# Softmax shifts with the logarithm of the row sum, taken on ScalarE ahead of the weighted sums, in a fused attention and FFN kernel

## The chip, the core and the metric

The kernel runs on one core of a Trainium2 chip. A core has TensorE (PE), VectorE (DVE), ScalarE (ACT), GpSimd (POOL) and SyncE (SP, which issues DMAs here); each works through its own list of instructions in order, and they meet only through semaphores. The metric is the time of one execution on the device in microseconds (us), lower is better. Some 0.3% (3.5 us) is about what a measurement of this kernel can tell.

## The reference, cut to what matters

```
x:(16,256,512)  ctx:(16,256,512)   HEADS=16, DK=32, WINDOW=128
q = rope(layernorm(x) @ wq.T);  k = rope(ctx @ wk.T);  v = ctx @ wv.T
scores = q @ k.T * sqrt(32), masked where |q - k| > 128
x = x + (softmax(scores) @ v) @ wo.T + wo_b
x = x + ffn(layernorm(x))      # W_in and W_out rounded to 8 bits, activations to 16; exact gelu
```

## The kernel before

**Phases.** Up to about 700 us of the profile the attention runs, 16 steps, one for each batch element b of 256 tokens; then the two FFN products. Only the attention is changed. All products there are done in split precision: an operand is a high part (rounded) and a low part (the rest), and `split3` makes three matmuls of each product. q and k of a head have 32 rows; high and low parts stand under one another (96 rows, `q_st`, `k_st`), so that one matmul gives scores of a head.

**A step.** `step(b)` on each engine is written out by hand, and this order is what runs. In a first half PE computes `scores(b, n)` for each head n (queries down the partitions), DVE masks them and takes each row's maximum (`row_maxima`, line 1224, two operations per head and a read of the result), and between them PE computes the projections of the next element: k (`qk_tile(b + 1, "k", ...)`, four pieces of 12 matmuls), the transposes of x (`x_transposes`, L529), V in two tiles of four triples (`v_tile`, L514 to L516), q (four pieces). Then the maxima are split and transposed (L620) and placed under the 96 rows of `q_st`, so that the same product subtracts them. In a second half PE computes the scores transposed (`scores_t`, L642), ACT takes the exponential (L973), POOL zeroes the corners outside the window (`band`, L1565), and after every four heads PE sums the values weighted (`weighted`, L656) and, with a one-hot operand, the denominators (`denominators`, L669). The output product of element b - 1 (`o_products`, 24 matmuls: for each half of the tokens eight with the high part, L589, and four with the low part, L593) is strewn through the end of the first half and the second half by `some(count)`.

**Denominators.** In the next step DVE inverts the sums (L1265), ACT issues two DMAs that spread them (`store_sums`, `spread_shares`), and DVE multiplies `oT` by them (L1271) before `ot_lead` (ACT, L950) and `ot_rest` (POOL, L1553) split it for the output product.

**Waits that matter.** PE has two score banks (`ring`): `scores(b, n)` waits until head n - 2 has left its bank. `v_tile(j, 0)` writes bank 6, which also holds the second half of x transposed, so it waits for `xt_lo`, the semaphore of `xt_rest` on DVE (L1257); `xt_rest` waits for `xt_lead` on ACT (L933). The k rotation on DVE (`rotate`, L1247 to L1250, three operations per half) ends in `roped`, from which ACT rounds k's high part (L913) and POOL makes the low part in four pieces (L1542); the part of `o_products` with the low part waits for `ot_rest`. The first thing that ACT does in a step is `norm1` (L929). SP stacks q and k by DMA when their parts are there.

## Time and profile before

| | |
|---|---|
| three runs | 1176.55 us median (1173.67 to 1177.44) |
| profiled execution | 1176.49 us, span of its instructions 1174.8 us |
| busy: PE, DVE, ACT, POOL | 1135.5 us (97%), 946.8 (81%), 646.8 (55%), 375.7 (32%) |
| granted TensorE clock, mean | 0.988 of full |
| chain that ended last, largest shares | PE 44%, DVE 26%, issue 25% |

A busy PE is not PE at its peak, since matmuls overlap: a row's length is the latency of one, and its pace is the distance of starts. The mean over the span also mixes the attention with the FFN phases, so one step of the attention has to be cut out.

### The profile page before, as it was taken

To read this page: it belongs to the slowest core of one execution; us is meant where nothing else is said; L and a number is where in the kernel's file an instruction comes from. 1 tells how busy PE (TensorE), PEld (TensorE's weight loads), DVE (VectorE), ACT (ScalarE), POOL (GpSimd) and SP (SyncE) were. 2 spreads that over 40 slices of the span, in tenths; PEclk is the share of its full clock that TensorE was granted. 3 is DMA by queue.
4 is the path that set the end of the run, shared out by engine and by line. 5 is a ranking of instruction groups with operands and counts; after the bars stand their busy time and mean duration, and the time that the engine had idled before them with its cause. 6 is when DMAs were issued, how large, how long until landed. Compare 5 with 4: busy or idle time off the path is not lost.

```text
span 1174.8 us, 23540 instructions
## 1 busy us (share of the span) xinstructions
PE 1135.5 (97%) x7928; PEld 766.9 (65%) x7928; DVE 946.8 (81%) x2413; ACT 646.8 (55%) x1033; POOL 375.7 (32%) x540
## 2 busy tenths in 40 slices
PE   6999999999999999999999789999999999999998
PEld 6867887887788788778878464444444444444443
DVE  6879989999999999999998756666666687777776
ACT  5255356436534643563464255555555577777774
POOL 1247337534743663474365230000000021111121
PEclk9989999999999999999999799999999999999999
DMA  8554674566457556646753723555553402676662
GB/s 281 133 150 114 172 221 118 148 184 163 126 175 212 129 137 184 172 123 179 203 139 92 222 65 118 197 196 198 196 196 117 152 1 77 214 232 227 224 216 99
DMA packets 100522, 191.10 MB, mean 163 GB/s; under 512 B 13376, under 2 KB 30912, under 8 KB 100416
## 3 DMA queue, kind: packets, MB, share of 16 engines
q1 hardware_dynamic: 96096, 179.92, 50.9%
q10 hardware_dynamic: 4320, 9.83, 2.8%
q8 instruction: 59, 0.97, 0.4%
q14 instruction: 47, 0.39, 0.1%
HBM read 89.16 MB, written 43.91 MB: 113 GB/s over the span
## 4 chain that ended last, share of the span: by engine, by line
PE 44%; DVE 26%; issue 25%; DMA 2%; ACT 1%; SPq 1%; DVEq 0%; POOL 0%; POOLq 0%; ACTq 0%
PE bank L864 19%; DVE bank L1224 12%; PE bank L642 6%; PE bank L656 5%; PE bank L669 5%; DVE row_max L1224 3%; PE bank L589 3%; PE bank L593 2%; DVE neg_max L1265 2%; DVE roped L1250 2%; DVE rt L1248 2%; DVE rt L1247 1%; DVE neg_max L1229 1%; DVE t_lo L1257 1%; PE bank L608 1%
## 5 line engine op out<-in xcount | busy, mean ns | idle before, releaser
L1224 DVE CUSTOM_DVE_ANT_0 bank<-bank,mask 128x256 f32<-128x256 f32 x512 | 203.5, 453 | 33.9 <-PE bank L608 23.1
L864 PE MATMUL bank<-wout_int,g_hi 128*128 128x512 bf16 x512 | 193.6, 379 | 0.1
L864 PE MATMUL bank<-wout_int,g_lo 128*128 128x512 bf16 x512 | 193.6, 379 | 0.0
L825 PE MATMUL bank<-qT_hi,win_int 128*128 128x512 bf16 x496 | 188.0, 379 | 0.0
L825 PE MATMUL bank<-qT_lo,win_int 128*128 128x512 bf16 x496 | 188.0, 379 | 0.0
L973 ACT ACTIVATE probs<-bank 128x512 f32<-128x512 f32 x256 | 139.0, 599 | 37.0 <-PE bank L642 31.1
L1542 POOL TENSOR_TENSOR k_lo<-roped,k_hi 128x256 fp32r<-128x256 f32 x60 | 55.0, 947 | 263.5 <-ACT k_hi L913 263.5
L1520 DVE TENSOR_TENSOR g_lo<-h_int,g_hi 128x512 f16<-128x512 f32 x128 | 89.1, 696 | 41.3 <-ACT g_hi L1129 37.4
L1565 POOL TENSOR_SCALAR_AFFINE_SELECT probs<-probs 128x256 f32<-128x256 f32 x256 | 107.1, 429 | 35.9 <-ACT probs L973 30.0
L1097 ACT ACTIVATE h_ring<-bank,b_in,g_scale 128x512 f32<-128x512 f32 x96 | 73.1, 779 | 71.2 <-PE bank L825 56.4
L1462 DVE TENSOR_REDUCE hmax<-h_ring 128x512 f32 (+1 forms) x96 | 63.1, 682 | 58.5 <-ACT h_ring L1097 56.4
L608 PE MATMUL bank<-k_st,q_st 96*128 96x256 f32 x512 | 94.6, 296 | 14.8 <-DVE row_max L1224 13.9
L642 PEld LDWEIGHTS bank<-q_st,k_st 128*128 128x128 f32 x512 | 87.3, 192 | 31.8 <-issue 13.2
L642 PE MATMUL bank<-q_st,k_st 128*128 128x256 f32 x512 | 102.7, 295 | 2.7 <-ACT probs L973 1.4
L1129 ACT CAST g_hi<-h_int 128x512 f16<-128x512 f32 x128 | 79.0, 617 | 47.2 <-PE bank L864 43.2
L608 PEld LDWEIGHTS bank<-k_st,q_st 96*128 96x128 f32 x512 | 78.1, 193 | 32.6 <-issue 22.0
L954 ACT COPY v_sb<-bank 128x512 f32<-128x512 f32 x32 | 18.8, 586 | 141.5 <-PE bank L516 141.5
L1608 POOL TENSOR_TENSOR xq<-xq,b_out 128x512 f32<-128x512 f32 x32 | 41.6, 1298 | 166.4 <-ACT h_int L1138 166.4
L864 PEld LDWEIGHTS bank<-wout_int,g_hi 128*128 128x128 f16 x512 | 50.0, 98 | 60.9 <-issue 0.6
L864 PEld LDWEIGHTS bank<-wout_int,g_lo 128*128 128x128 f16 x512 | 50.1, 98 | 60.3 <-DVE g_lo L1520 0.2
L825 PEld LDWEIGHTS bank<-qT_hi,win_int 128*128 128x128 bf16 x496 | 48.5, 98 | 57.8 <-ACT h_ring L1097 0.3
L825 PEld LDWEIGHTS bank<-qT_lo,win_int 128*128 128x128 bf16 x496 | 48.5, 98 | 57.6
(170 smaller groups left out, 2735.0 us busy)
## 6 DMA issues: line engine op xcount, KB each, us to landing
hidden_scratch<-h_ring SPq DMA_DIRECT2D x96, 256.0 KB, 2.1
h_ring<-hidden_scratch SPq DMA_DIRECT2D x96, 256.0 KB, 2.9
k_st<-k_hi SPq DMA_DIRECT2D x128, 128.0 KB, 2.9
q_st<-q_hi SPq DMA_DIRECT2D x128, 128.0 KB, 2.7
xq<-x_scratch SPq DMA_DIRECT2D x16, 1024.0 KB, 6.0
x_ln<-in_x SPq DMA_DIRECT2D x16, 512.0 KB, 6.3
ctx_raw<-in_ctxT SPq DMA_DIRECT2D x16, 512.0 KB, 5.0
k_st<-k_lo SPq DMA_DIRECT2D x64, 128.0 KB, 2.8
```

What stands on the lines that cost most here:

```text
L608: mm = pe.matmul(ring[n % 2][:, qb * S:(qb + 1) * S], q_st[0:MROW, n, qb * P:(qb + 1) * P], k_st[0:MROW, n], start=True, stop=True)
L642: mm = pe.matmul(third[n][:, kb * S:(kb + 1) * S], k_st[:, n, kb * P:(kb + 1) * P], q_st[:, n], start=True, stop=True)
L656: mm = pe.matmul(pv_bank[i // 2][DK * c:DK * (c + 1), (i % 2) * S:(i % 2 + 1) * S], v_sb[:, par, kb, n], probs[:, n % SLOTS, kb], start=kb ...
L825: mm = pe.matmul(bank[f % 4][:], win_int[:, c, f * P:(f + 1) * P], part[:, par, c], start=c == 0 and part is qT_hi, stop=c == KC - 1 and p ...
L864: return pe.matmul(bank[4 * par + u][:], part[:, f % 4, u * P:(u + 1) * P], wout_int[:, f], start=f == 0 and part is g_hi, stop=f == FC - ...
L973: act.activation(probs[:, n % SLOTS].rearrange("p k q -> p (k q)"), third[n][:], ACT.Exp, scale=SCORE_SCALE).then_inc(exp_done, 1)
L1097: act.activation(dst, bank[f % 4][:], ACT.Gelu, bias=b_in[:, f:f + 1], scale=g_scale[:, f:f + 1]).then_inc(gelu_done, 1)
L1129: act.copy(g_hi[:, f % 4], h_int[:, f % 4]).then_inc(ghi_done, 1)
L1224: dve.tensor_tensor_reduce(sc, sc, mask[:, (1 - qb) * P:(1 - qb) * P + S], 1.0, NEG, ALU.add, ALU.max, row_max[:, qb, n:n + 1]).then_inc(m ...
L1462: dve.tensor_reduce(hmax[:, bass.ds(FC * n + f, 1)], src, AX_X, ALU.max, apply_absolute_value=True).then_inc(hmax_done, 1)
L1520: dve.tensor_tensor(g_lo[:, f % 4], h_int[:, f % 4], g_hi[:, f % 4], ALU.subtract).then_inc(glo_done, 1)
L1565: pool.affine_select(out=far, in_=far, compare_op=ALU.is_ge, fill=0.0, base=1 - P, pattern=[[0, 2], [1, P]], channel_multiplier=1).then_in ...
```

## The change

Three things are changed in the attention; the FFN is as it was.

**Row sums in the first half.** `wq` is scaled by minus the score scale, so scores come out negated and the maximum is a minimum (`row_minima`). ACT then exponentiates the masked scores of each head in place, with the row's minimum as bias, and takes the sum over the row as an accumulator output (`row_sums`, two operations of 256 columns per head). Behind the last head ACT takes the logarithm of the sums and one exponential for a correction step (`logs`), and DVE forms minimum and logarithm together in five short operations (`log_sums`). The transposed shift then holds both, so the exponentials of the second half are the probabilities themselves.

**No denominators.** The one-hot matmuls, the inversion, the two DMAs, the multiplications and, at the end, `last_shares` go.

**Order.** PE has one projection piece behind each head; the second V tile has two triples behind heads 11 and 12 and two in the second half; six output products stand behind heads 13 and 14, 12 ahead of the transposes, 4 behind them, 2 later. Scores now wait for ACT's sum (`sum_done`), not for DVE's maximum. On DVE the weight quantising stands behind heads 0 to 2, the x rests behind heads 4 and 5 and the six operations of the k rotation behind heads 6 to 11, one each. The high part of k goes from ACT to POOL (`k_lead`), the low part of q from POOL to DVE (`q_low`), and `bias_x` stands first on POOL; its `ctx_lo` parts stand behind heads 8 to 11. ACT has `xt_lead` behind head 3, a V copy behind 7, `ot_lead` behind 11, and the second V copy and the ctx cast among the exponentials.

```diff
@@ PE, scores @@
-                    pe.wait_ge(max_done, 2 * (H * b + n - 1))
+                    pe.wait_ge(sum_done, 2 * (H * b + n - 1))
...
@@ PE, clump @@
                 for kb in range(2):
-                    weighted(b, par, i, kb)
-                for kb in range(2):
-                    denominators(b, i, kb, has_proj)
+                    weighted(b, par, i, kb, has_proj)
...
 # PE, step
-                    tiles[1] += [lambda: qk_tile(b + 1, "k", 0)]
-                    tiles[3] += [lambda: x_transposes(b + 1, 0), lambda: x_transposes(b + 1, 1), lambda: qk_tile(b + 1, "k", 1, (0,))]
-                    tiles[5] += [lambda: qk_tile(b + 1, "k", 1, (1,)), lambda: v_tile(b + 1, 0, range(2))]
-                    tiles[7] += [lambda: v_tile(b + 1, 0, range(2, KC)), lambda: qk_tile(b + 1, "q", 0, (0,))]
...
+                    for n, (which, half, col) in {0: ("k", 0, 0), 1: ("k", 0, 1), 3: ("k", 1, 0), 4: ("k", 1, 1),
+                                                  7: ("q", 0, 0), 8: ("q", 0, 1), 9: ("q", 1, 0), 10: ("q", 1, 1)}.items():
+                        tiles[n] += [lambda which=which, half=half, col=col: qk_tile(b + 1, which, half, (col,))]
+                    tiles[2] += [lambda: x_transposes(b + 1, 0), lambda: x_transposes(b + 1, 1)]
+                    tiles[5] += [lambda: v_tile(b + 1, 0, range(2))]
+                    tiles[6] += [lambda: v_tile(b + 1, 0, range(2, KC))]
+                    tiles[11] += [lambda: v_tile(b + 1, 1, range(1))]
+                    tiles[12] += [lambda: v_tile(b + 1, 1, range(1, 2))]
+                for n in (13, 14):
+                    tiles[n] += [lambda: some(3)]
...
-                some(7)
+                some(12)
                 max_transposes(b, has_proj)
                 some(4)
...
 # ACT
+            def row_sums(b, n):
+                if n == 0:
+                    wait(act, lse_chain, LSE_OPS * b)
+                act.wait_ge(min_done, 2 * (H * b + n + 1))
+                for qb in range(2):
+                    sc = ring[n % 2][:, qb * S:(qb + 1) * S]
+                    act.activation(sc, sc, ACT.Exp, scale=-1.0, bias=row_min[:, qb, n:n + 1],
+                                   accum_out=row_sum[:, qb, n:n + 1]).then_inc(sum_done, 1)
+            def logs(b):
+                act.wait_ge(sum_done, 2 * H * (b + 1))
+                act.activation(lse[:], row_sum[:], ACT.Ln).then_inc(log_done, 1)
+                act.wait_ge(log_done, 2 * b + 1)
+                act.activation(lse_e[:], lse[:], ACT.Exp, scale=-1.0).then_inc(log_done, 1)
...
+                for n in range(H):
+                    row_sums(b, n)
+                    if n == 3 and has_proj:
+                        xt_lead(b + 1, 0)
+                        xt_lead(b + 1, 1)
+                    if n == 7 and has_proj:
+                        v_copy(b + 1, 1 - par, 0)
+                    if n == 11 and has_o:
+                        ot_lead(b - 1, 0, has_proj)
+                        ot_lead(b - 1, 1, has_proj)
+                logs(b)
...
 # DVE, step
+                for n in (0, 1, 2):
+                    between[n] += [lambda: next(window, None)]
+                    between[4] += [lambda: xt_rest(b + 1, 0)]
+                    between[5] += [lambda: xt_rest(b + 1, 1)]
+                    for n in (6, 7, 8):
+                        between[n] += [lambda: next(first, None)]
+                    for n in (9, 10, 11):
+                        between[n] += [lambda: next(second, None)]
...
 # POOL, step
+                if has_o:
+                    bias_x(b - 1)
                 if has_proj:
+                    k_lead(b + 1)
                     for c in range(KC):
                         split_lo("k", b + 1, c)
                 if has_o:
                     ot_rest(b - 1, 0)
                     ot_rest(b - 1, 1)
-                    bias_x(b - 1)
...
                 for n in range(H):
                     band(b, n)
-                    if 6 <= n < 10 and has_proj:
-                        split_lo("q", b + 1, n - 6)
+                    if 8 <= n < 12 and has_xt:
+                        ctx_lo(b + 2, n - 8)
```

Three places in the order of the instructions follow. The first is PE at the first V piece of a middle step, before the change; bank 6 is the one of the V tile, and the rows ahead are the last of the k tile.

```order
L514 MATMUL bank3<-cT_hi,wk_hi 128x256
L515 MATMUL bank3<-cT_lo,wk_hi 128x256
L516 MATMUL bank3<-cT_hi,wk_lo 128x256
L514 MATMUL bank6<-wv_hi,cT_hi 128x512 [waits xt_lo,oT_out]
L515 MATMUL bank6<-wv_lo,cT_hi 128x512
L516 MATMUL bank6<-wv_hi,cT_lo 128x512
```

The same place of the changed kernel.

```order
L510 MATMUL bank3<-cT_hi,wk_lo 128x256
L600 MATMUL bank1<-k_st,q_st 128x256 [waits sum_done]
L600 MATMUL bank1<-k_st,q_st 128x256
L508 MATMUL bank6<-wv_hi,cT_hi 128x512 [waits xt_lo,oT_out]
L509 MATMUL bank6<-wv_lo,cT_hi 128x512
L510 MATMUL bank6<-wv_hi,cT_lo 128x512
```

The V piece has moved directly behind the scores of head 5, in bank 1; its wait for `xt_lo` is the same.

DVE in a middle step, before the change, at the x rests (`t_lo`), which stand behind the maxima of heads 2 and 3.

```order
L1224 ISA bank,row_max<-bank,mask 128x256 [waits s_mm]
L1224 ISA row_max 128x1
L1224 ISA bank,row_max<-bank,mask 128x256
L1224 ISA row_max 128x1
L1257 TENSOR_TENSOR t_lo<-bank,t_hi 128x4x128 [waits xt_hi] x2
L1224 ISA bank,row_max<-bank,mask 128x256 [waits s_mm]
```

The same in the changed kernel, from the second operation of head 4 on.

```order
L1200 ISA bank,row_min<-bank,mask 128x256
L1200 ISA row_min 128x1
L1249 TENSOR_TENSOR t_lo<-bank,t_hi 128x4x128 [waits xt_hi]
L1200 ISA bank,row_min<-bank,mask 128x256 [waits s_mm]
L1200 ISA row_min 128x1
L1200 ISA bank,row_min<-bank,mask 128x256
L1200 ISA row_min 128x1
L1249 TENSOR_TENSOR t_lo<-bank,t_hi 128x4x128 [waits xt_hi]
```

The first rest now stands behind head 4 and the second behind head 5.

POOL in a middle step before the change, from the low parts of k to the first selects.

```order
L1542 TENSOR_TENSOR k_lo<-roped,k_hi 128x256 [waits k_hi_done]
L1542 TENSOR_TENSOR k_lo<-roped,k_hi 128x256 x3
L1553 TENSOR_TENSOR t_lo<-oT,t_hi 128x4x128 [waits ot_hi] x2
L1558 TENSOR_TENSOR x_res<-x_res,wo_b 128x512 [waits xres_in]
L1558 TENSOR_TENSOR x_res<-x_res,wo_b 128x512
L1548 TENSOR_TENSOR cT_lo<-ctx_raw,cT_hi 128x256 [waits c_hi]
L1548 TENSOR_TENSOR cT_lo<-ctx_raw,cT_hi 128x256
L1565 AFFINE_SELECT probs<-probs 128x256 [waits exp_done] x2
```

The same stretch of the changed kernel.

```order
L1549 TENSOR_TENSOR x_res<-x_res,wo_b 128x512 [waits xres_in]
L1549 TENSOR_TENSOR x_res<-x_res,wo_b 128x512
L1533 CAST k_hi<-roped 128x1024 [waits k_stacked2,k_stacked1,k_stacked3,k_stacked0,rope_k_step]
L1527 TENSOR_TENSOR k_lo<-roped,k_hi 128x256 [waits k_hi_done]
L1527 TENSOR_TENSOR k_lo<-roped,k_hi 128x256 x3
L1544 TENSOR_TENSOR t_lo<-oT,t_hi 128x4x128 [waits ot_hi] x2
L1556 AFFINE_SELECT probs<-probs 128x256 [waits exp_done] x9
```

The bias has moved ahead of everything, a cast of k stands before its low parts, and `ot_rest` (`t_lo`) still follows them.

## Rows read from the trace of the kernel before

**Rows 1.** Timeline of DVE: start us, length us, engine, line, what, xcount.
```profile
305.83 1.08 DVE L1229 TENSOR_SCALAR neg_max<-row_max 128x32 fp32r<-128x32 f32 x1
...
632.38 1.07 DVE L1229 TENSOR_SCALAR neg_max<-row_max 128x32 fp32r<-128x32 f32 x1
```

**Rows 2.** Timeline of PE, one step of the attention phase.
```profile
302.45 0.41 PE L608 MATMUL bank<-k_st,q_st 96*128 96x256 f32 x2
...
307.19 0.44 PE L620 MATMUL bank<-ident,neg_max 128*128 128x128 f32 x2
...
312.70 1.07 PE L656 MATMUL bank<-probs,v_sb 128*32 128x256 f32 x16
313.59 1.05 PE L669 MATMUL bank<-probs,hot 128*32 128x256 f32 x16
...
323.74 0.74 PE L608 MATMUL bank<-k_st,q_st 96*128 96x256 f32 x4
324.32 0.28 PE L514 MATMUL bank<-cT_hi,wk_hi 128*128 128x256 f32 x1
...
327.15 0.64 PE L608 MATMUL bank<-k_st,q_st 96*128 96x256 f32 x4
327.62 1.04 PE L529 MATMUL bank<-ident,x_ln 128*128 128x128 f32 x8
...
331.81 0.40 PE L514 MATMUL bank<-wv_hi,cT_hi 128*128 128x512 f32 x1
...
333.21 0.64 PE L608 MATMUL bank<-k_st,q_st 96*128 96x256 f32 x4
```

**Rows 3.** Timeline of DVE, the same step.
```profile
303.04 0.43 DVE L1224 CUSTOM_DVE_ANT_0 bank<-bank,mask 128x256 f32<-128x256 f32 x1
...
303.77 0.14 DVE L1224 DVE_READ_ACCUMULATOR2_ANT row_max<- 128x1 f32 x1
...
325.93 1.75 DVE L1265 RECIPROCAL neg_max<-bank 128x256 f32<-128x256 f32 x1
...
329.24 1.28 DVE L1257 TENSOR_TENSOR t_lo<-bank,t_hi 128x512 fp32r<-128x512 f32 x2
...
337.06 0.69 DVE L1250 TENSOR_TENSOR roped<-rt 128x512 f32<-128x512 f32 x1
```

**Rows 4.** Timeline of ACT; in brackets idle us before, and its releaser.
```profile
318.60 2.07 ACT L973 ACTIVATE probs<-bank 128x512 f32<-128x512 f32 x4 [1.10 <-PE bank L642]
...
323.01 0.59 ACT L943 COPY oT<-bank 128x512 f32<-128x512 f32 x1 [0.49 <-PE bank L656]
...
323.97 1.53 ACT L929 ACTIVATE x_ln<-x_ln,nmr,rstd 128x512 f32<-128x512 f32 x2
...
337.78 1.05 ACT L913 CAST k_hi<-roped 128x1024 fp32r<-128x1024 f32 x1 [1.90 <-DVE roped L1250]
...
647.54 1.38 ACT L961 ACTIVATE rt<-x_res,mv 128x512 f32<-128x512 f32 x2
...
693.70 0.62 ACT L950 CAST t_hi<-oT 128x512 fp32r<-128x512 f32 x1 [2.85 <-DVE oT L1386]
```

**Rows 5.** Timeline of POOL.
```profile
53.04 2.83 POOL L1542 TENSOR_TENSOR k_lo<-roped,k_hi 128x256 fp32r<-128x256 f32 x4 [16.15 <-ACT k_hi L913]
...
301.82 2.54 POOL L1553 TENSOR_TENSOR t_lo<-oT,t_hi 128x512 fp32r<-128x512 f32 x2
...
316.99 0.41 POOL L1565 TENSOR_SCALAR_AFFINE_SELECT probs<-probs 128x256 f32<-128x256 f32 x1
317.37 0.73 POOL L1542 TENSOR_TENSOR q_lo<-roped,q_hi 128x256 fp32r<-128x256 f32 x1
```

**Rows 6.** PE timeline, then stretches: PE, PEld, DVE, ACT, POOL busy, PEclk, DMA, GB/s.
```profile
61.98 2.17 PE L642 MATMUL bank<-q_st,k_st 128*128 128x256 f32 x8 [0.93 <-ACT q_st L966]
...
60.00:65.00 5.00, 3.14 (x12) 2.48 (x13) 4.79 (x11) 4.47 (x8) 3.33 (x5) 0.71 0.29 69
65.00:70.00 5.00, 5.00 (x43) 2.99 (x42) 4.43 (x11) 3.00 (x5) 4.92 (x10) 0.60 0.73 167
```

249 lines of the change are left out of this document (99 added, 150 removed).

## Prediction

> **What bounds the kernel now.** I read the page first: TensorE (PE) is busy for 97% of the span and VectorE (DVE) for 81%. Then I cut one step of the attention phase out of the timelines. Steps are equal: the statement that ends a first half runs at 305.83 and, eight steps later, at 632.38 [rows 1], so a step is 40.82 us. There are 16, of which 14 (b = 1 to 14) hold everything.
>
> A step has two halves. The first runs from scores of head 0 (323.74) to the transposes of the maxima, at 307.19 one step earlier, which is 348.01 in this one [rows 2]: 24.27 us. The second is the other 16.55 us. PE is nearly solid in both. A k or q piece is 12 matmuls; 24 take 2.83 us (324.32 to 327.15), so a piece is 1.41; a V piece of six 512-column matmuls is 1.40 (331.81 to 333.21), so a 512-column matmul is 0.233; two scores are 0.24; the eight x transposes 0.80 [rows 2]. PE is the limit, DVE is close behind it in the first half, and ScalarE (ACT) and POOL have slack. So what matters is where PE is made to wait.
>
> **What the change removes from PE.** The denominators: four clumps of the size of a weighted sum's, 0.89 us (312.70 to 313.59): 3.6 us per step [rows 2]. DVE loses the reciprocal (1.75) and the multiplications by it [rows 3]. None of this counts if the order holds PE up elsewhere, so I walk one middle step, with t = 0 at scores of head 0.
>
> **Prices.** From the start of two scores to the start of the reduction on DVE 0.59 us (302.45 to 303.04); a head on DVE 0.87 (to 303.91) [rows 2, 3]; a rotation operation or x rest 0.69 latency, 0.64 each in a pair [rows 3]. An exponential of 512 columns on ACT has a pitch of 0.49 (four in 2.07). The row sum is not in the trace. `centre`, with one per-partition operand and 512 columns, has a pitch of 0.64 (two in 1.38, one 0.74); 256 columns less, at 0.83 ns each, give 0.43 pitch and 0.53 latency, so 0.96 a head [rows 4]. Bounds: 0.80 (nothing for the operand), and 1.25 if reading out each sum costs what DVE's 0.14 read does [rows 3]. I take 0.96. The Trainium skill (ScalarE: Activation LUTs, What ACT_TABLE_LOAD costs) gives an ACTIVATE with a pointer bias 280 ns plus 0.833 ns per column and an overlap of 93 ns: by that an estimate of 0.89 a head, and the sum would be the same, since ACT is not last.
>
> **ACT enters late.** Behind the last weighted sum ACT still has two copies (0.96 together) and the two normalisations (1.53) before the first row sums, and starts them 0.2 us after t = 0 [rows 4]. So sums of head 0 run 2.6 to 3.6, and scores of head 2, which now wait for them, start at 3.7 instead of 3.3. Cost 0.4.
>
> **The V piece waits for x.** Head 2: transposes to 4.7; head 3 to 6.4; head 4 to 8.0; scores of head 5 at 8.0 to 8.3. Now the V piece (bank 6) still needs `xt_lo`, that is `xt_rest` of both halves, and the second one stands on DVE behind `row_minima(5)`, which needs those very scores (the pieces of the order of PE and DVE show both). ACT: sums 3 to 7.8, `xt_lead` to 8.8. DVE: first rest 8.35 to 9.0, minima of head 5 from 9.05 to 9.9, second rest to 10.5. PE begins V at 10.6: 2.3 us idle. Even with nothing else late it is 0.59 + 0.77 + 0.64 + 0.1 - 0.24 = 1.9. In before both rests were done at 330.5 and V began at 331.8 [rows 2, 3].
>
> **The rotation ends late.** Heads 6 to 10 follow at 12.0, 13.7, 15.3, 17.0, 18.6 (0.24 + 1.4 each), head 11 at 20.3. DVE does one of the six k rotation operations behind each head from 6 to 11, so the last, which completes `roped`, ends at 20.3 + 0.59 + 0.77 + 0.69 = 22.3. Before, it ended at 337.75, which is t = 14.0 [rows 3].
>
> **POOL comes last.** Behind `roped` POOL now has, in this order, the cast of k to its high part, four low parts, and only then `ot_rest`, on which the ninth output product waits. Four k_lo take 2.83 uncontended (they took that in step 0), one `ot_rest` 1.27 [rows 5]. The cast of 1024 columns on POOL is not in the trace: a one-input select of 256 has a pitch of 0.38, so about 1.3 for four times that; bounds 1.05 (what ACT needs for it [rows 4]) and 2.5 (the two-input rate of 1.27 for 512). Then t_lo of half 0 is there at 22.3 + 1.3 + 2.8 + 1.3 + 0.1 = 27.8. PE meanwhile: `ot_lead` stands on ACT behind sums of head 11 (22.7) and holds sums of 12 to 24.7 and so scores of 14 to 24.8; scores of 15 at 25.8; products 7 and 8 to 26.5; then it waits to 27.8. The ten products up to the transposes take 2.33: t = 30.2. The other branch, minima and sums of head 15 (28.2), two logarithm steps and four short DVE operations, is ready at about 29.5, up to 29.9 where DVE is held up by POOL as at 305.83 (1.08 us for 32 columns [rows 1]). The first half grows from 24.3 to **30.2**.
>
> **The second half.** ACT starts the two copies of the maxima behind the transposes (0.44 [rows 2]). Two V triples (0.7 each) and four products stand between the first scores, so exponential 0 starts at 1.8 and about 0.7 more is lost before exponential 4. Up to exponential 8 ACT has nine of them at 0.49, and now the V copy (0.5) and the ctx cast beside the q cast (1.0 each [rows 4]): it ends at 9.3, and exponential 15, with the small root steps between, at 13.2. POOL has nine selects and then a ctx low part behind each of heads 8 to 11: 1.06 us per pair [rows 5], so select 15 ends at 9.3 + 4.2 + 1.6 = 15.1; the last clump 0.9: **15.9** (16.5 to 14.7 if POOL is 0.6 slower or not last). DVE's whole `q_low` (about 1.2) ends near 10.0; three DMAs later q is stacked before the next scores. Gain 0.6.
>
> **Sum.** A middle step is 30.2 + 15.9 = 46.1, 5.3 more than 40.8; times 14 is +74. Step 0 has the V wait and no product to cover the logarithms: +3. Step 15 has heads held to about 1.1 us by scores, minima and sums through two banks: +1. Behind it the share products go, for which ACT waited 2.85 us [rows 4]: -3.5. The profiled run took 1176.5 us (span 1174.8), as good as the median of 1176.55; so 1176.5 + 74 + 0.5 = **1251**.
>
> **Rivals.** (a) *Forecast*, chance 0.55, own range 1218 to 1290: with sums at 0.80, the cast at 1.05 and select 15 hidden a step is 44.3 (1225); with the cast at 2.5 and sums at 1.25 it is 48.8 (1289).
> (b) *PE's clock falls in the new gaps*, 0.20. In step 0 PE had gaps of some 0.9 us around its transposes (the second ends at 61.98), and the granted clock was 0.71 and 0.60 in the mean of the next two stretches of 5 us [rows 6]; between full speed and the lower level, 0.5 or 1.2 GHz, that is 2.9 + 4.0 = 6.9 us at the lower. The new gaps are 2.3 and 1.3 us with dense work around them, so it may happen or not. Where PE sets the pace a fall costs half of its length, 3.4 us at most, where ACT does almost nothing: 2 to 3.4 a step, +28 to +48, 1279 to 1299. The Trainium skill (TensorE: Matmul & The Clock Gate, HAM oscillation) says that waits in every iteration can throttle the clock each time; by that rule it would be about 1290, and the trace of before does not decide it for gaps of this size.
> (c) *ACT bounds*, 0.06: if a row sum is far dearer than 0.6 (one accumulator read of 0.2 us or more each), ACT needs over 1.5 a head and 24 us for 16, plus 4 of casts: first half 32, 1275.
> (d) *The waits are shorter than I think, but do not vanish*, 0.08: step of 41 to 43.5, 1180 to 1214.
> (e) *Faster*, 0.07: the removed work shows. PE's own work in the new first half is 24.7; with a second half of 14.7 set by ACT a step is 39.4, 1.4 less: 1154. It decides from the V wait: this needs `xt_rest(1)` before t = 8.3 and POOL's t_lo before 24, against rows that put them at 10.5 and 27.8. For it speaks only that PE, DVE and POOL all have less to do.
> (f) *No change*, 0.04: a step of 40.8, half of the waits hidden.
>
> Faster, the same and slower by more than 0.3% (some 3.5 us, what a measurement tells here): 0.08, 0.04, 0.88. The range takes in (a), (b) to its upper edge and part of (d): 1205 to 1310.
>
> **What would show it.** PE idle before L508 wv at head 5, about 2 us, released by DVE t_lo; PE idle before the low output products, released by POOL t_lo; k_hi on POOL some 22 us after scores of head 0; two L956 in about 1 us; first half near 30 us. Wrong if PE stays solid through a first half of 25 us, if POOL casts k in under 0.6 us, or if the granted clock is under 1 in every step.

## The result, and the profile after

| | before | after |
|---|---|---|
| median (lowest to highest) | 1176.99 us (1173.67 to 1179.1) | 1281.3 us (1278.45 to 1286.33), four runs each |
| ratio after / before | | 1.0904, 95% interval 1.0879 to 1.0929 |
| span of the profiled execution | 1174.8 us | 1280.3 us |
| mean granted TensorE clock | 0.988 | 0.972 |

The changed kernel is 9% slower. Of the runs behind experiments 5 to 8, two of the kernel before (1636 and 2307 us) and one of experiment 7 (4731 us) fell in a slow state of the chip; every ratio below leaves them out.

The page of after, busy time first, then its costliest groups that the change brought or touched:

```profile
PE 1128.5 (88%) x6844; PEld 748.3 (58%) x6888; DVE 906.8 (71%) x2427; ACT 879.4 (69%) x2074; POOL 337.0 (26%) x495
...
L956 ACT ACTIVATE bank<-bank,row_min 128x256 f32<-128x256 f32 x512 | 228.2, 446 | 140.8 <-DVE row_min L1200 138.8
...
L600 PE MATMUL bank<-k_st,q_st 96*128 96x256 f32 x512 | 118.7, 315 | 28.5 <-ACT bank L956 27.4
...
L956 ACT ACTIVATION_READ_ACCUMULATOR bank<-bank,row_min 128x1 f32 x512 | 102.9, 201 | 0.0
L647 PE MATMUL bank<-probs,v_sb 128*32 128x256 f32 x1024 | 69.9, 391 | 34.9 <-POOL probs L1556 26.4
```

DVE and POOL lost busy time, ACT gained 233 us, and PE's share fell from 97 to 88%: nobody is the bound, everybody waits. ACT, which gained most, has the larger idle column (140.8 us, for minima); it is not what paces the kernel. What does is to be read from a step.

**Where the 105.5 us of span lie.** The end of each first half is marked by one statement on DVE: the split of the maxima in before, the cast of the shifts in after. First, fifteenth and sixteenth of them; before (the fifteenth is in [rows 1]):

```profile
60.15 0.18 DVE L1229 TENSOR_SCALAR neg_max<-row_max 128x32 fp32r<-128x32 f32 x1
...
670.00 1.03 DVE L1229 TENSOR_SCALAR neg_max<-row_max 128x32 fp32r<-128x32 f32 x1
```

and after:

```profile
69.98 0.18 DVE L1212 CAST shift<-lse_z 128x32 fp32r<-128x32 f32 x1
...
738.87 0.18 DVE L1212 CAST shift<-lse_z 128x32 fp32r<-128x32 f32 x1
...
782.79 0.18 DVE L1212 CAST shift<-lse_z 128x32 fp32r<-128x32 f32 x1
```

Up to the first mark: 9.8 us more. The fourteen intervals of middle steps: 668.9 against 572.2, that is 96.7 more. The last interval: 43.9 against 37.6, 6.3 more. From the last mark to the end: 497.5 against 504.8, 7.3 less. Together 105.5.

**One middle step of after.** PE's timeline from a first scores of head 0 to the next (a row: start, length, engine, line, names, count, and in brackets the idle time before it and what ended it):

```profile
326.93 0.50 PE L600 MATMUL bank<-k_st,q_st 96*128 96x256 f32 x2
...
335.05 0.40 PE L600 MATMUL bank<-k_st,q_st 96*128 96x256 f32 x2
337.40 0.47 PE L508 MATMUL bank<-wv_hi,cT_hi 128*128 128x512 f32 x1 [1.96 <-DVE t_lo L1249]
...
351.64 0.50 PE L600 MATMUL bank<-k_st,q_st 96*128 96x256 f32 x2 [0.48 <-ACT bank L956]
...
354.41 1.20 PE L585 MATMUL bank<-wo_hi,t_lo 128*128 128x512 f32 x4 [0.72 <-POOL t_lo L1544]
...
356.88 0.44 PE L612 MATMUL bank<-ident,shift 128*128 128x128 f32 x2
...
366.10 0.51 PE L630 MATMUL bank<-q_st,k_st 128*128 128x256 f32 x2 [0.69 <-ACT probs L940]
...
370.41 1.07 PE L647 MATMUL bank<-probs,v_sb 128*32 128x256 f32 x16 [1.17 <-POOL probs L1556]
...
372.54 1.07 PE L647 MATMUL bank<-probs,v_sb 128*32 128x256 f32 x16 [0.73 <-POOL probs L1556]
373.54 0.50 PE L600 MATMUL bank<-k_st,q_st 96*128 96x256 f32 x2
```

First half 29.95 us (356.88 - 326.93; before 24.27, [rows 2]), second 16.66 (before 16.55): 46.61 in all. The rows show where TensorE stands idle: at the V piece for DVE's x rest, at head 14 for ACT's sums, at the ninth output product for POOL's low part, in the second half for ACT's exponentials, and ahead of the last two clumps for POOL's selects. With those that are cut out here (0.39 us at head 13; 0.56, 0.35 and 0.21 us for exponentials) the waits of the first half are 3.55 us and those of the second 3.71. Before the change the rows of the second half name no wait of TensorE at all. Its work in that half fell by the 3.6 us of the denominators and by another 1.2 (an estimate: eleven output products of 0.233 us moved out, two V triples of 0.7 moved in), and the half is as long as it was: what was taken out has become waits. The transposes (L612) show no idle time, but the shifts were ready only 0.05 us before them:

```profile
353.41 0.43 DVE L1200 CUSTOM_DVE_ANT_0 bank<-bank,mask 128x256 f32<-128x256 f32 x1 [0.20 <-PE bank L600]
...
355.63 0.19 DVE L1208 TENSOR_TENSOR lse_z<-lse,row_min 128x32 f32<-128x32 f32 x1 [1.35 <-ACT lse L961]
355.97 0.19 DVE L1210 TENSOR_TENSOR lse_t<-row_sum,lse_e 128x32 f32<-128x32 f32 x1
...
356.64 0.19 DVE L1213 TENSOR_TENSOR shift<-lse_z,shift 128x32 fp32r<-128x32 f32 x1
```

So two branches end together, within 0.05 us: POOL's low part with the ten products behind it, and minima, sums and logarithms of head 15.

**The other length.** Of the fourteen intervals three last 46.5 to 46.6 us, ten 48.05 to 48.74, one 47.5. The longer ones show this behind the V wait:

```profile
192.88 0.47 PE L508 MATMUL bank<-wv_hi,cT_hi 128*128 128x512 f32 x1 [1.96 <-DVE t_lo L1249]
...
193.91 0.63 PE L509 MATMUL bank<-wv_lo,cT_hi 128*128 128x512 f32 x1
194.34 0.63 PE L510 MATMUL bank<-wv_hi,cT_lo 128*128 128x512 f32 x1
...
196.90 0.57 PE L509 MATMUL bank<-wv_lo,cT_hi 128*128 128x512 f32 x1
197.31 0.39 PE L510 MATMUL bank<-wv_hi,cT_lo 128*128 128x512 f32 x1
```

Starts lie 0.43 us apart instead of 0.233 for some 3.4 us, and the granted clock of the 10 us around it is 0.83: TensorE ran at 1.2 instead of 2.4 GHz there. It costs 1.5 us (48.07 - 46.52). Nine of the fourteen intervals have such a fall behind V; of the two others that are long, the first has the lower clock at its start and the last one on the first heads.

### The profile page after: what moved, and what is told of

Same layout as the page of the kernel before. It is cut to its first block, busy times and chain, and to the rows that moved or that the text cites. A ratio compares the mean times of both kernels' runs of the same rounds, so it can differ in the third digit from the quotient of the medians.

```text
span 1280.3 us, 22334 instructions
## 1 busy us (share of the span) xinstructions
PE 1128.5 (88%) x6844; PEld 748.3 (58%) x6888; DVE 906.8 (71%) x2427; ACT 879.4 (69%) x2074; POOL 337.0 (26%) x495
## 4 chain that ended last, share of the span: by engine, by line
PE 41%; issue 23%; DVE 14%; ACT 10%; POOL 10%; DMA 1%; DVEq 0%; POOLq 0%; SPq 0%; ACTq 0%
PE bank L829 17%; DVE bank L1200 6%; PE bank L508 5%; PE bank L509 4%; PE bank L510 4%; ACT probs L940 4%; POOL k_lo L1527 3%; PE bank L600 3%; POOL cT_lo L1539 3%; PE bank L581 2%; POOL probs L1556 2%; ACT bank L956 2%; PE bank L585 2%; PE bank L647 2%; PE bank L630 1%
## 5 line engine op out<-in xcount | busy, mean ns | idle before, releaser
L956 ACT ACTIVATE bank<-bank,row_min 128x256 f32<-128x256 f32 x512 | 228.2, 446 | 140.8 <-DVE row_min L1200 138.8
L829 PE MATMUL bank<-wout_int,g_hi 128*128 128x512 bf16 x491 | 185.8, 379 | 0.4 <-ACT g_hi L1105 0.2
L790 PE MATMUL bank<-qT_hi,win_int 128*128 128x512 bf16 x474 | 179.6, 379 | 0.0
L1556 POOL TENSOR_SCALAR_AFFINE_SELECT probs<-probs 128x256 f32<-128x256 f32 x256 | 115.6, 464 | 121.1 <-ACT probs L940 118.2
L600 PE MATMUL bank<-k_st,q_st 96*128 96x256 f32 x512 | 118.7, 315 | 28.5 <-ACT bank L956 27.4
L600 PEld LDWEIGHTS bank<-k_st,q_st 96*128 96x128 f32 x512 | 85.5, 201 | 66.5 <-ACT bank L956 44.5
L1105 ACT CAST g_hi<-h_int 128x512 f16<-128x512 f32 x128 | 79.0, 617 | 47.2 <-PE bank L829 43.2
L630 PEld LDWEIGHTS bank<-q_st,k_st 128*128 128x128 f32 x512 | 76.8, 192 | 54.6 <-ACT probs L940 23.5
L956 ACT ACTIVATION_READ_ACCUMULATOR bank<-bank,row_min 128x1 f32 x512 | 102.9, 201 | 0.0
L647 PE MATMUL bank<-probs,v_sb 128*32 128x256 f32 x1024 | 69.9, 391 | 34.9 <-POOL probs L1556 26.4
L1549 POOL TENSOR_TENSOR x_res<-x_res,wo_b 128x512 f32<-128x512 f32 x32 | 40.3, 1281 | 213.2 <-DMA x_res<-in_x 213.2
```

Of the source, the lines that this page charges most:

```text
L600: mm = pe.matmul(ring[n % 2][:, qb * S:(qb + 1) * S], q_st[0:MROW, n, qb * P:(qb + 1) * P], k_st[0:MROW, n], start=True, stop=True)
L630: mm = pe.matmul(third[n][:, kb * S:(kb + 1) * S], k_st[:, n, kb * P:(kb + 1) * P], q_st[:, n], start=True, stop=True)
L647: mm = pe.matmul(pv_bank[i // 2][DK * c:DK * (c + 1), (i % 2) * S:(i % 2 + 1) * S], v_sb[:, par, kb, n], probs[:, n % SLOTS, kb], start=kb ...
L790: mm = pe.matmul(bank[f % 4][:], win_int[:, c, f * P:(f + 1) * P], part[:, par, c], start=c == 0 and part is qT_hi, stop=c == KC - 1 and p ...
L829: return pe.matmul(bank[4 * par + u][:], part[:, f % 4, u * P:(u + 1) * P], wout_int[:, f], start=f == 0 and part is g_hi, stop=f == FC - ...
L956: act.activation(sc, sc, ACT.Exp, scale=-1.0, bias=row_min[:, qb, n:n + 1], accum_out=row_sum[:, qb, n:n + 1]).then_inc(sum_done, 1)
```

## Experiments

All kernels are the changed one with an edit; "1281" is the changed kernel itself, ratio 1.0904 to the kernel before. The ratio of each run is again to the kernel before.

**1. Fill the gap.** In the changed kernel TensorE works through the wait.

```diff
@@ PE, v_tile; FILLS is 18 @@
+                if s == 0 and chunks[0] == 0 and not (isinstance(j, int) and j == 0):
...
+                        wait(pe, oT_out, 2 * (j - 1))
+                    keep_busy(pv_bank[1], FILLS)
                 if s == 0:
                     pe.wait_ge(xt_lo, 2 * j + 2)
```

> The changed kernel, with 18 matmuls of 256 columns, whose results nobody reads, on TensorE ahead of the wait for the x rests at head 5 (some 1.9 us, in a bank that stands free), so that the engine works through the gap; the wait itself stays, and so do the sums of a step. Theory A (the gap costs its 2 us of waiting, and besides that TensorE's clock falls to the lower level behind it in some 11 of 14 steps, which costs 1.5 us in each of them): the steps of 48.05 us become steps of 46.5 to 46.7, the granted clock is 1.00 in the 10 us behind V in every step, and the time falls from 1281 to about 1264 us. Theory B (the clock falls for another reason, such as the load of that stretch): the falls and the steps of 48.05 stay, time 1280 to 1285. Theory C (steps of 48 are not the clock's: the order of waits makes them): clock 1.00 and the time unchanged.

Measured: 1272.0 us, ratio 1.0823 (1.0773 to 1.0872). Of the fourteen intervals the first is 48.5 us, the next nine are 46.5 to 46.9 and the last four 47.8 to 47.9. Stretches of 10 us (PE, PEld, DVE, ACT, POOL busy, then PEclk, DMA share, GB/s): V in one step, and the start of a late step:

```profile
190.00:200.00 10.00, 10.00 (x74) 9.37 (x73) 7.25 (x26) 5.47 (x21) 2.55 (x2) 1.00 0.25 93
...
550.00:560.00 10.00, 9.49 (x74) 8.29 (x75) 5.89 (x25) 5.75 (x17) 0.45 (x2) 0.83 0.99 272
```

With the gap filled the clock holds at V, in every middle step, and the wait itself still costs its time. So the gap causes the fall there (theory A), and theory C is out. Yet in the last four middle steps the clock fell at another place, on the first heads of a step, behind the waits at the last clumps. Hence 9 us gained where theory A had 17. A kernel with several gaps has several places for a fall.

**2. x rests earlier.**

```diff
@@ PE @@
-                    for n, (which, half, col) in {0: ("k", 0, 0), 1: ("k", 0, 1), ...
+                    for n, (which, half, col) in {0: ("k", 0, 0), 2: ("k", 0, 1), ...
-                    tiles[2] += [lambda: x_transposes(b + 1, 0), lambda: x_transposes(b + 1, 1)]
+                    tiles[1] += [lambda: x_transposes(b + 1, 0), lambda: x_transposes(b + 1, 1)]
@@ ACT @@
-                    if n == 3 and has_proj:
+                    if n == 2 and has_proj:
                         xt_lead(b + 1, 0)
@@ DVE @@
-                    between[4] += [lambda: xt_rest(b + 1, 0)]
-                    between[5] += [lambda: xt_rest(b + 1, 1)]
+                    between[3] += [lambda: xt_rest(b + 1, 0)]
+                    between[4] += [lambda: xt_rest(b + 1, 1)]
```

> The changed kernel, with the x transposes behind head 1 instead of 2 (the second k piece behind head 2), the two ScalarE casts of x behind the sums of head 2 instead of 3, and the two rests on VectorE behind the minima of heads 3 and 4 instead of 4 and 5. Theory A (the gap at the V piece is the second rest behind the minima of a head whose scores stand ahead of V, and everything of the first half behind it is late by that gap): TensorE's wait at V falls from 2.0 to under 0.4 us, no fall of the clock behind it, roped is complete 2 us sooner after the scores of head 0, the first half goes from 29.95 to about 28.0 us and a middle step to 44.5: 1281 - 15 x 2.0 - 11 x 1.5 = about 1235 us. Theory B (another limit stands right behind the gap: POOL's cast and low parts or the chain of the logarithms): the gap goes and the time comes back as a longer wait at the low output products or at the transposes; step 46 to 46.5 and time 1262 to 1270, only the clock's part gained.

Measured: 1248.5 us, ratio 1.0630 (1.0604 to 1.0655). PE of one step:

```profile
538.88 0.51 PE L600 MATMUL bank<-k_st,q_st 96*128 96x256 f32 x2
...
541.56 1.09 PE L523 MATMUL bank<-ident,x_ln 128*128 128x128 f32 x8 [0.53 <-ACT x_ln L894]
...
549.51 0.40 PE L600 MATMUL bank<-k_st,q_st 96*128 96x256 f32 x2
...
565.05 1.20 PE L585 MATMUL bank<-wo_hi,t_lo 128*128 128x512 f32 x4 [0.85 <-POOL t_lo L1544]
...
567.49 0.38 PE L612 MATMUL bank<-ident,shift 128*128 128x128 f32 x2
```

Scores of head 6 come 10.63 us behind those of head 0 instead of 11.95, and the transposes 28.61 instead of 29.95: what the V wait gives back, 1.3 us, arrives at the end of the half in full, and an interval is 45.2 to 45.3 us in nine of fourteen. 0.53 of the gap lives on as a wait of the transposes for ACT's `norm1`. The clock falls only in two middle steps. 15 x 1.3 and eight falls fewer at 1.5 make 31.5, and 32.8 were measured. Theory A in its mechanism; it had promised 46, for it had the gap go whole and the clock with it everywhere.

**3. POOL's low part of oT first.**

```diff
@@ POOL @@
+                if has_o:
+                    ot_rest(b - 1, 0)
+                    ot_rest(b - 1, 1)
                 if has_proj:
                     k_lead(b + 1)
                     for c in range(KC):
                         split_lo("k", b + 1, c)
-                if has_o:
-                    ot_rest(b - 1, 0)
-                    ot_rest(b - 1, 1)
```

> The changed kernel, with POOL's two low parts of oT ahead of the cast of k and its four low parts, instead of behind them. Theory A (of the two branches that meet at the transposes of the shifts, POOL's low part holds the ninth product up by 0.7 us, but the chain minima, sums, logarithms of head 15 ends last, at 29.9): the wait for POOL at the ninth product is gone and the same time stands before the transposes as a wait for VectorE's last operation; first half shorter by 0.3 us at most, time 1276 to 1283 us. Theory B (POOL's branch sets the end, as the prediction had it): the first half is shorter by 0.7 us or more, time 1270 or less. Theory C: POOL's k_lo end later, run into the first selects of the second half and hold the first weighted sums: time over 1285.

Measured: 1284.1 us, ratio 1.0945 (1.0908 to 1.0982), no gain. The wait for POOL at the ninth product is gone, and one for DVE stands ahead of the transposes. PE, and DVE ahead of it:

```profile
594.61 0.44 PE L612 MATMUL bank<-ident,shift 128*128 128x128 f32 x2 [1.51 <-DVE shift L1213]
...
592.72 0.49 DVE L1208 TENSOR_TENSOR lse_z<-lse,row_min 128x32 f32<-128x32 f32 x1 [1.35 <-ACT lse L961]
593.24 0.65 DVE L1210 TENSOR_TENSOR lse_t<-row_sum,lse_e 128x32 f32<-128x32 f32 x1
```

Both took 0.19 in after; now POOL's k_lo run beside them (591.03 to 593.84). Intervals without a fall are 47.2 instead of 46.5. So with POOL's branch out of the way the chain of the logarithms ends last, and POOL's order makes it later by slowing its small operations. Taking away the wait for POOL alone gains nothing. That is theory A's mechanism, though the half grew by 0.5 us, which it did not have. Which of the two branches was the last in the changed kernel this does not tell; there they end together.

**4. Low parts of ctx two heads sooner.** `if 6 <= n < 10 and has_xt: ctx_lo(b + 2, n - 6)` instead of `8 <= n < 12` and `n - 8`, on POOL.

> The changed kernel, with POOL's four low parts of ctx behind the selects of heads 6 to 9 instead of 8 to 11. Theory A (in the second half POOL comes last: its pairs of select and low part have a pitch of 1.06 us against 0.5 of the exponentials, and TensorE waits 1.2 and 0.7 us for its selects before the last clumps): POOL starts its pairs two heads sooner and catches up behind them, the two waits shrink by 0.6 to 1.1 us together, time 1281 - 15 x 0.8 = about 1268 us (1264 to 1273). Theory B (ScalarE's exponentials or the stacking of q would set the end anyway): the waits change their name to ScalarE and the time stays within 3 us of 1281. Theory C: the select of head 7 comes later and holds the second clump, and with it the ring of banks: time over 1285.

Measured: 1275.6 us, ratio 1.0838 (1.0802 to 1.0874). The group of weighted sums between 150 and 700 us, in after and in this run (busy, mean ns, idle before and its releasers):

```profile
L647 PE MATMUL bank<-probs,v_sb 128*32 128x256 f32 x720 | 48.2, 384 | 27.8 <-POOL probs L1556 21.0 <-ACT probs L940 6.8
```

```profile
L647 PE MATMUL bank<-probs,v_sb 128*32 128x256 f32 x736 | 49.3, 384 | 20.0 <-POOL probs L1556 12.8 <-ACT probs L940 6.8
```

The wait for POOL is 8.2 us less over some 11.5 steps: 0.7 a step, and intervals with a fall are 47.37 instead of 48.07, one without is 45.83 instead of 46.52. POOL comes last in the second half (theory A). The time fell by 6 and not by 10, because now all but one of the intervals have a fall, where eleven had.

**5. Without reading the sums.** `accum_out` left out of `row_sums`, `row_sum` a constant: the kernel leaves out the true sums, but the same 512 exponentials run.

> The changed kernel without the accumulated output of the first exponentials: the same 512 ScalarE instructions over 256 columns, but no row sum is read out (the sums are a constant 64.0 in every row, so the kernel leaves that part of the softmax out). Theory A (in a middle step ScalarE is not last; only its last part, sums of head 15 into the logarithms, and the pace of the last step hang on it): the second ACTIVATION_READ_ACCUMULATOR of a head goes, the pitch of two exponentials falls from 0.90 to 0.75 to 0.80 us, the chain of the logarithms ends 0.2 to 0.4 us sooner, middle steps are 0.2 to 0.4 us shorter and the last interval about 1.5 us: time 1281 - 5 = 1276 us (1270 to 1279). Theory B (the row sums on ScalarE pace the first half): a step is shorter by 16 x 0.1 us or more, time 1255 or less. Theory C: the read is free beside the next exponential, no change at all, 1281.

Measured: 1280.2 us, ratio 1.0899 (1.0862 to 1.0935): no gain. ACT's timeline, first the changed kernel with its read, then this run:

```profile
329.44 0.44 ACT L956 ACTIVATE bank<-bank,row_min 128x256 f32<-128x256 f32 x1
329.80 0.20 ACT L956 ACTIVATION_READ_ACCUMULATOR bank<-bank,row_min 128x1 f32 x1
329.89 0.45 ACT L956 ACTIVATE bank<-bank,row_min 128x256 f32<-128x256 f32 x1
```

```profile
300.40 1.55 ACT L956 ACTIVATE bank<-bank,row_min 128x256 f32<-128x256 f32 x4
```

Four exponentials in 1.55 us are a pitch of 0.37 instead of 0.45, so the read costs some 0.08 us of pace each, 2.6 us of ACT per step. The last interval fell from 43.9 to 42.0 us. Theory C's time, by another reason: intervals became shorter by 0.15 to 0.2 us, but some two more of them had a fall of the clock. 2.6 us less of ACT's work in a step bring 0.15, so ACT's throughput does not pace the first half, and rival (c) of the prediction is out. That covers the read alone: no run takes the 32 exponentials of a step away, so what their place in the chain from scores to scores costs is not measured.

**6. The denominators' time put back.** 32 unused matmuls of 256 columns per step behind the clumps.

```diff
@@ PE, clump @@
+                if has_proj and i < NC4 - 1:
...
+                    keep_busy(q_bank[1], 16 if i == NC4 - 2 else 8)
```

> The changed kernel, with as many matmuls of 256 columns as the denominators had before (8 behind the first and the second weighted clump, 16 behind the third, 32 in a step, some 3.5 us), whose results nobody reads. It puts back on TensorE the time that the change took away. Theory A (the second half is set by ScalarE's exponentials and POOL's selects, so that the removed work was under a cover of waits and bought nothing): middle steps grow by 0 to 1 us, and with TensorE busier the clock may fall in fewer of them: 1272 to 1297 us. Theory B (the removed work is worth its time, and the change would have been 50 us slower without it): steps grow by 2.5 to 3.5 us, time 1318 to 1333.

Measured: 1284.2 us, ratio 1.0936 (1.0897 to 1.0974), 3 us above the changed kernel for some 52 us of PE work, a difference no larger than what a measurement can tell; the intervals say more. Intervals are 47.5 where the clock holds, 1.0 more, and the clock falls in three of them (one is the first) instead of in eleven. PE, end of a step:

```profile
560.30 1.07 PE L647 MATMUL bank<-probs,v_sb 128*32 128x256 f32 x16 [0.40 <-POOL probs L1560]
561.31 1.92 PE L675 MATMUL bank<-win_int 128*128 128x256 bf16 x16
```

The waits at the clumps shrank (0.40 us for the third, 1.17 in the changed kernel; none for the fourth, 0.73 there): the unused work stands in them. So the removed work, 3.5 us a step, was worth 1.0 us in this order, and with the work back in place eight fewer falls of the clock, some 12 us, pay for most of that. One difference to the denominators: their last part stood behind the fourth clump, here it stands ahead of it. From the waits either place costs about the same, an estimate: 1.75 us of work less a wait of 0.73 here, 0.88 less 0.73 and 0.88 more there.

**7. and 8. Orders for both halves, and for the first alone.** 7 has the edits of 2 and 3, `ot_lead` behind head 10, and:

```diff
@@ PE @@
+                    tiles[13] += [lambda: v_tile(b + 1, 1, range(2, 3))]
+                    tiles[14] += [lambda: v_tile(b + 1, 1, range(3, KC))]
...
-                some(12)
+                some(18)
                 max_transposes(b, has_proj)
...
-                    if n in (0, 2) and has_proj:
-                        v_tile(b + 1, 1, range(2 + n // 2, 3 + n // 2))
@@ ACT @@
                 logs(b)
+                if has_proj:
+                    v_copy(b + 1, 1 - par, 1)
+                if has_xt:
+                    ctx_hi(b + 2)
                 max_copy(b, 0, slice(0, 2))
...
-                    if n == 4 and has_proj:
-                        v_copy(b + 1, 1 - par, 1)
-                    if n == 5 and has_xt:
-                        ctx_hi(b + 2)
-                    if n == 7 and has_proj:
+                    if n == 6 and has_proj:
                         split_hi("q", b + 1)
@@ POOL @@
+                if has_xt:
+                    for c in range(KC):
+                        ctx_lo(b + 2, c)
                 for n in range(H):
                     band(b, n)
-                    if 8 <= n < 12 and has_xt:
-                        ctx_lo(b + 2, n - 8)
```

8 has all of this but the last lines of ACT and POOL, from `logs` on: its second half is that of the changed kernel.

> The changed arithmetic in another order. x transposes behind head 1, casts behind the sums of head 2, rests behind the minima of 3 and 4 (as in the run before); the cast of oT behind the sums of head 10 instead of 11 and POOL's low parts of it ahead of those of k; all V triples behind heads 11 to 14 and 18 output products behind head 15, to cover the chain of the logarithms; ScalarE's copy of V and the cast of ctx while it waits for the transposes, POOL's low parts of ctx ahead of the first select, and the cast of q behind exponential 6. Theory A (the loss is a matter of order, not of the work: the waits that the runs showed are 1.3 us at V, 1.5 to 2 at the chain of head 15 and 2 to 3 behind ctx in the second half): first half 26.6 to 27.5 us, second 12.5 to 14, middle step 39.5 to 41.3, time 1281 - 15 x 6 - 15 of clock = about 1170 us, 1155 to 1190, that is at or a little under the kernel before. Theory B (the row sums' chain through two score banks bounds the first half, and the stacking of q and k by DMA the second): first half over 28 and second over 15, time 1215 to 1250.

> The same order as e7_reordered in the first half alone; the second half is the changed kernel's (copy of V, casts of ctx and q behind exponentials 4, 5 and 7, low parts of ctx behind selects 8 to 11). Against the run with earlier x rests (1248.5 us, first half 28.6, second 16.6) it tells what the cover of the logarithms is worth. Theory A: first half 26.6 to 27.5 us, second half 15.5 to 16.5 (two V triples less between its first scores), middle step 42.5 to 43.7, time 1210 to 1228 us. Theory B (the chain is not covered, TensorE waits for the shifts as before, or the second half grows by what the first loses, since POOL and the casts set it): step 44.5 or more, time 1240 to 1250.

Measured: 7: 1242.4 us, ratio 1.0571 (1.0522 to 1.0619); 8: 1248.3 us, 1.0641 (1.0587 to 1.0694), the same as experiment 2. In 8 the transposes no longer wait, but come 28.97 us behind scores of head 0: the two V triples and six products that cover the chain now fill the half (from 563.51, scores of head 15, to 568.06, without a gap). Moved work is not removed. And the second half kept 16.4 us with less of PE's work in it: ACT and POOL set it (theory B of 8). In 7 the last clump ended 13.4 us after the transposes (560.11), 3.3 sooner, and then:

```profile
572.63 0.83 PE L647 MATMUL bank<-probs,v_sb 128*32 128x256 f32 x12
575.50 0.47 PE L600 MATMUL bank<-k_st,q_st 96*128 96x256 f32 x2 [2.04 <-issue]
```

The scores of head 0 waited for the stacked q, whose DMAs stood behind `q_low` on DVE (568.96 to 570.4). This is the longest such wait; in eight of the middle steps it is some 0.6 us and the second half is 14.0 us. The larger loss lies in the first half: 30.2 to 31.7 us in all but two of the middle steps. Its longest wait, 1.2 to 2.5 us in most steps, is at the scores of head 3. DVE, then PE:

```profile
578.54 0.69 DVE L1261 TENSOR_REDUCE w_s<-w_raw 128x1 f32<-128x512 f32 x1 [1.50 <-DMA w_raw<-in_winT]
...
581.61 0.51 PE L600 MATMUL bank<-k_st,q_st 96*128 96x256 f32 x2 [1.40 <-ACT bank L958]
```

The first part of the quantising stands behind head 0 on DVE and waits for the window's DMA, which SP issues behind the DMAs of q; minima and sums of head 1, and so the scores of head 3, wait with it. Theory B by its time and its first half, but by a wait that it did not name.

**10. All orders.** 7, with `q_low` ahead of `ln1_stats` on DVE, the cast of q behind exponential 4, the quantising behind heads 2, 5 and 12, and in the last step 5 unused matmuls behind each of heads 0 to 12. **11. The last two of these alone** in the changed kernel.

> The order of e7_reordered, whose first half took 24.3 us, as before the change, but where the next scores of head 0 waited 2.0 us for the stacked q behind a late q_low. Changed against it: ScalarE's cast of q behind exponential 4 instead of 6, q_low on VectorE ahead of the statistics of the next x, the three parts of the quantising behind the minima of heads 2, 5 and 12 instead of 0, 1 and 2 (in the last step their DMA is late), and in the last step 5 matmuls of 256 columns behind each of heads 0 to 12, whose results nobody reads, to hold the clock. Theory A (the stacking of q was all that was left in the second half): second half 13.4 to 14 us, first half 24.5 to 26, middle step 38.0 to 40.0, last interval 2 to 3 us shorter, time 1242 - 14 x 6 - 3 = about 1155 us (1145 to 1176), faster than the kernel before. Theory B (the sums on ScalarE begin late behind casts and norms, and the first half grows by what the second loses): first half 26.5 us or more, step over 41, time 1185 to 1215.

> The changed kernel, with only the three parts of the quantising behind the minima of heads 2, 5 and 12, and in the last step alone 5 matmuls of 256 columns behind each of heads 0 to 12, whose results nobody reads. It asks why the last interval grew by 6.3 us where the prediction had 1. Theory A (a wait for the window's DMA on VectorE holds the sums of head 1 by 2.8 us, and the chain scores, minimum, sum runs at the lower clock of a TensorE that stands idle): the interval from the fifteenth to the sixteenth transposes falls from 43.9 us by 2.5 to 4.5, middle steps stay: time 1276 to 1280. Theory B (the pace of that step is that of DVE and ScalarE through two banks alone): it stays within 1 us of 43.9.

Measured: 10: 1219.3 us, ratio 1.0381 (1.0359 to 1.0402), middle step 43.6: second half 14.39, first 29.2. Neither wait of 7 is left, for the stacked q or at head 3, and the clock falls only at the start of the first interval. The time lies above both theories; the first half is as theory B has it, by a cause that it did not name: TensorE has some 26 us of its own work there (an estimate: the prediction's 24.7 and the two V triples that moved in) and waits of 0.53, 0.65 and 0.39 us. The expectation said that the first half of 7 took 24.3 us; that is the half of the kernel before, and 7 had 30.2 and more, so a half of 24.5 to 26 had no ground. 11: 1302.5 us, ratio 1.1086 (1.1058 to 1.1114). Its last interval is 39.9 us instead of 43.9, so the late quantising (DVE waits 1.88 us for the window's DMA in after, and TensorE 3.28 us at head 3, row below) and the lower clock of an idle TensorE made that interval long (theory A there); the run changes both, and which of the two made more was not tried. Middle steps, though, grew by 1.4 us: the second part of the quantising stands behind head 5 ahead of `xt_rest(1)`, and V waits that much longer. Rows of PE, after:

```profile
759.89 0.80 PE L600 MATMUL bank<-k_st,q_st 96*128 96x256 f32 x2 [3.28 <-ACT bank L956]
```

and a middle step of 11:

```profile
545.02 0.47 PE L508 MATMUL bank<-wv_hi,cT_hi 128*128 128x512 f32 x1 [3.03 <-DVE t_lo L1253]
```

Heads 6 to 12 all come 1.1 us later for the 1.07 us more of wait; another 0.2 us come at head 15, behind the third part of the quantising. So the V wait is on the path, as in 2. The middle intervals are 24 us longer together, as more of them have a fall too, and the last is 4 shorter: 21 us above the changed kernel, where theory A had 1 to 5 below. The miss is this edit's side effect.

**12. Tuned further, and 13. the same with the denominators' time back.** 12 is 10 with q's cast on POOL behind the fourth select, 16 and 6 products around the transposes instead of 18 and 4, the second `ot_lead` behind head 12.

> The run with all orders (1219 us, middle step 43.6: first half 29.2, second 14.4) with three more moves: the cast of q to its high part on POOL behind the fourth select instead of on ScalarE among the exponentials; 16 instead of 18 output products ahead of the transposes of the shifts and 6 instead of 4 behind them; the second of ScalarE's two casts of oT behind the sums of head 12, the first stays behind head 10. Theory A (the second half is set by ScalarE: two copies, sixteen exponentials at 0.49 and the cast; the first by TensorE's own work of some 26 us and 3 us of short waits): second half 13.4, first half 28.3 to 28.8, middle step 41.8 to 42.3, time 1219 - 14 x 1.5 = about 1198 us (1190 to 1204), still above the kernel before. Theory B (POOL as a third engine at its limit: low parts of ctx, selects and the cast of q in one row hold the clumps, and q is stacked late): step 43.6 or more, 1219 to 1235.

> The kernel of e12_tuned with 32 matmuls of 256 columns per step, whose results nobody reads, behind the weighted clumps, as in e6_denominators_back, where they cost nothing (1284 against 1281). Theory A (the second half is now nearer to TensorE's own work: 9.5 us of it in some 13.4, and the three clumps stand right ahead of exponentials that wait for scores): a step is 0.5 to 2 us longer, time 7 to 28 us above e12_tuned. Theory B (still under the cover of the exponentials): within 4 us of e12_tuned. Theory C (its whole length shows): 48 us more.

Measured: 12: 1226.9 us, ratio 1.0450 (1.0432 to 1.0467), middle step 44.2, worse than 10. 13: 1252.4 us, 1.0669 (1.0651 to 1.0686), middle step 45.75. In 12 ACT's small root of the layer norm stands among the exponentials behind number 10, and waits for statistics that stand on DVE behind `q_low`, which now comes later:

```profile
519.37 0.20 ACT L893 ACTIVATE nt_t<-veps 128x2 f32<-128x2 f32 x1 [1.73 <-DVE veps L1156]
```

Five exponentials stand behind it; in 10 this wait was 0.63 in most steps. TensorE's wait for an exponential there is 0.78 us instead of 0.36, and one of 0.62 for a select of POOL, which now has the cast of q ahead of it, takes the place of one of 1.02 for ACT. And the transposes wait again for the shifts, 0.6 us, with two products less to cover them. The second half is 14.66 us (14.39 in 10), the first 29.55 (29.22). Theory B of 12 in its number; its late q does not show, and that the small operation in the wrong place is the cause, more than POOL, is read from rows and not tried. 13 answers 6: in a tighter order the same unused work costs 1.54 us a step, 25.5 us in all, where it cost 3; 12 has hardly a fall of the clock left that the work could win back, as it did in 6. The removed work gains worth only as the waits over it go.

## Why the prediction was right

It had 1251 us with a range of 1205 to 1310; 1281.3 came, a growth of 104 us where 74 were forecast. The path was right at nearly every place; too small was the term of 74 us for the middle steps, which had nothing for the clock.

- **ACT enters late, the V wait, the pace of heads.** Scores of head 2 at t = 3.6 (said 3.7), of head 5 at 8.1 (8.0), of head 6 at 11.95 (12.0), of head 11 at 20.2 (20.3). The idle time at V is 1.96 (2.3 said, 1.9 at the least), with the V piece at 10.5 (10.6). Right; the first steps of the walk were almost exact, and experiments 2 and 11 show that this wait is on the path.
- **Row sums.** 0.90 of pace per head against 0.96. Right, though made otherwise: the operation is shorter and a read of its own stands behind it. Experiment 5: the read is not on the path. By the Trainium skill (ScalarE: Activation LUTs, What ACT_TABLE_LOAD costs) the estimate was 0.89. That this is so close is luck: it took off one overlap for the two operations; back to back each has one, and the estimate by the same figures is 0.80. Measured are 0.90 with the reads and 0.74 without them (experiment 5).
- **Rotation and POOL.** `roped` at 22.2 (22.3); cast of k 1.04 us, the low bound of 1.05, not the 1.3 that I took; t_lo at 27.4 (27.8).

```profile
349.20 1.04 POOL L1533 CAST k_hi<-roped 128x1024 fp32r<-128x1024 f32 x1 [6.59 <-DVE roped L1234]
```

The prediction let this branch end the half at 30.2, with the logarithms ready ahead of it at 29.5 to 29.9; in fact both were ready at 29.9 and the transposes came at 29.95. The wait for POOL was 0.72 (0.85 in most steps), not 1.3, and experiment 3 shows that removing it gives nothing. The total was right; that POOL's branch alone sets it was not.

- **Second half.** 15.9 said, 16.66 measured; POOL's pairs at 1.06 and the selects last, as said, and experiment 4 bears it out. Exponential 8 was to end at 9.3, and select 8 starts there. The missing 0.7 is mostly this select: 0.97 us instead of 0.4, while DVE's whole `q_low` ran beside it. That the one slows the other is read from the rows and was not tried.

```profile
365.69 1.23 DVE L1244 TENSOR_TENSOR q_lo<-roped,q_hi 128x1024 fp32r<-128x1024 f32 x1 [0.47 <-ACT q_hi L878]
...
366.21 0.97 POOL L1556 TENSOR_SCALAR_AFFINE_SELECT probs<-probs 128x256 f32<-128x256 f32 x1 [1.02 <-ACT probs L940]
```

- **The step.** 46.1 said; 46.5 where the clock holds, 46.6 in the one shown. The term of 74 us for 14 steps measured 79 (14 x 46.52 - 572.2).
- **The clock, rival (b).** It was put beside the forecast as an alternative at 0.20, and came true together with it: in eleven of fourteen intervals, but 3.4 us long instead of 6.9, and so 1.5 us dear against 2 to 3.4. That is the larger part of the miss of 30 us: 96.7 - 79.1 = 17.6 us. The range held the result because it was drawn to take rival (b) in; the sum had nothing for it. The rows of step 0 before the change [rows 6] had shown that gaps of some 0.9 us between dense work let it fall. That gaps in every step can let the clock fall in every step is what the Trainium skill has (TensorE: Matmul & The Clock Gate, HAM oscillation); here it did so in most steps, not in all. Experiment 1 shows the cause: filled, the same gap brings no fall. A gap behind which the rows of before show a fall should be a part of the likeliest case, with a share of the steps.
- **Edges.** The terms +3, +1 and -3.5 measured +9.8, +6.3 and -7.3. In step 0 the transposes waited 3.66 us for the logarithms with no output product to cover them, at the lower clock. For the last step the prediction had neither the window's late DMA ahead of the sums nor the clock of an idle TensorE (experiment 11, which changes both, gives back 4.0 of the 6.3). At the end 3.8 us more went than the share products' wait; what they were was not looked into.
- **Rivals (c), (d), (e), (f).** ACT as the bound is ruled out by its pace of 0.90 a head and by 5; shorter waits, no change and a faster kernel by the result. Experiment 6 measured what (e) hoped for: the removed work is worth 1.0 us a step in this order.

No order tried beats the kernel before: the best, experiment 10, is 3.8% above it. Why its first half needs 29.2 us is only read from its rows (some 26 us of TensorE's work by the estimate above, and waits of which the rows name 1.6 us) and was not tested. What the change of arithmetic costs apart from its order is not measured either, since no run has the old arithmetic in the new order; whether another order of this arithmetic gets below 1177 stays open.
